# Attention body of a macaron block: ScalarE's high-part copies set back by half a key tile and more, odd chunks' loads and reciprocals a body ahead

## The reference, cut to what matters

```
x = x + 0.5 * ffn(layernorm(x))
x = x + attn(layernorm(x))
x = x + 0.5 * ffn(layernorm(x))
# attn: 32 query heads of 16 over 8 key/value heads, signs of the weights as weights
scores = einsum('bhqd,bhkd->bhqk', q, k) / sqrt(16);  out = softmax(scores) @ v
y = einsum(out, sign(o_weight)) * (s * o_scale);  nan_to_num(y, posinf=1e6, neginf=-1e6)
# ffn: x @ W_base.T + b_base + top-2-of-8 LoRA experts
```

## Time and profile before

| what | value |
| --- | --- |
| median of 3 runs | 1164.61 us (1161.82 to 1164.77) |
| profiled execution, time | 1162.41 us |
| its span | 1160.6 us |
| mean granted TensorE clock | 0.957 of 2.4 GHz |
| busy: PE, DVE, ACT, POOL | 1064.6, 837.7, 726.6, 295.9 us |

### The profile page before, as it was taken

How to read it: one execution, slowest core, us unless ns; L and a number is a source line. 1 busy time by engine, 2 the same in 40 slices (tenths; PEclk the granted TensorE clock), 3 DMA queues, 4 the chain that set the end, 5 groups by cost and what they waited for, 6 DMA issues and landing times.

```text
span 1160.6 us, 16020 instructions
## 1 busy us (share of the span) xinstructions
PE 1064.6 (92%) x5776; PEld 468.4 (40%) x5776; DVE 837.7 (72%) x1107; ACT 726.6 (63%) x1361; POOL 295.9 (25%) x485
## 2 busy tenths in 40 slices
PE   5989887999999999999999999999999999998647
PEld 4778661344334432333334333433343334233336
DVE  5766679767776777776888688777877887871274
ACT  5556433757865786675676667666766675768321
POOL 5356546302410250410050024003200320041010
PEclk9989886999999998999999999999999999999869
DMA  7122331021211123011311120121113110301300
GB/s 254 37 90 89 99 104 48 27 74 35 63 36 40 33 60 111 30 32 35 101 31 31 55 81 31 31 87 48 31 31 106 31 38 23 105 12 34 115 0 37
DMA packets 70507, 68.31 MB, mean 59 GB/s; under 512 B 15132, under 2 KB 52508, under 8 KB 70428
## 3 DMA queue, kind: packets, MB, share of 16 engines
q1 hardware_dynamic: 70172, 67.15, 18.8%
q10 hardware_dynamic: 256, 0.13, 0.0%
HBM read 41.95 MB, written 24.63 MB: 57 GB/s over the span
## 4 chain that ended last, share of the span: by engine, by line
PE 73%; DVE 13%; ACT 5%; issue 3%; POOL 3%; DMA 1%; SPq 1%; ACTq 0%; DVEq 0%; POOLq 0%
PE ps_out L1524 19%; PE ps_score L1512 18%; PE ps_max L1493 16%; PE ps_fill L1449 5%; DVE neg_max L1320 5%; PE ps_fill L1478 3%; ACT probs L1018 2%; PE ps_fill L1431 2%; PE ps_fill L1453 1%; DVE neg_max L1117 1%; DVE zd L1191 1%; PE ps_fill L1417 1%; PE ps_out L1449 1%; PE ps_fill L1423 1%; PE ps_score L1449 1%
## 5 line engine op out<-in xcount | busy, mean ns | idle before, releaser
L1018 ACT ACTIVATE probs<-ps_score 128x512 f32<-128x512 f32 x992 | 538.9, 597 | 263.4 <-PE ps_score L1512 262.3
L1320 DVE TENSOR_REDUCE neg_max<-ps_max 128x1 f32<-128x1024 f32 x480 | 570.6, 1218 | 181.1 <-PE ps_max L1493 179.1
L1512 PE MATMUL ps_score<-qst,kst 99*128 99x512 bf16 x992 | 309.5, 387 | 9.8 <-ACT probs L1018 8.2
L1493 PE MATMUL ps_max<-kst,qst 96*128 96x512 bf16 x1024 | 289.7, 389 | 16.8 <-DVE neg_max L1117 5.9
L1524 PE MATMUL ps_out<-probs,v_ring 128*32 128x512 f32 x2048 | 275.3, 609 | 7.1 <-ACT o_sb L1027 4.7
L1512 PEld LDWEIGHTS ps_score<-qst,kst 99*128 99x128 bf16 x992 | 76.2, 97 | 274.6 <-ACT probs L1018 231.7
L1493 PEld LDWEIGHTS ps_max<-kst,qst 96*128 96x128 bf16 x1024 | 91.1, 99 | 143.9 <-issue 18.7
L852 POOL CAST shift<-neg_max 128x16 bf16<-128x16 f32 x32 | 9.5, 298 | 436.7 <-DVE neg_max L1320 432.3
L1524 PEld LDWEIGHTS ps_out<-probs,v_ring 128*32 128x32 f32 x2048 | 41.0, 108 | 96.0 <-issue 87.6
L948 ACT ACTIVATE xn<-xc,ln_shift,rstd 128x512 f32<-128x512 f32 x48 | 38.6, 814 | 30.9 <-POOL ln_shift L748 19.9
L1449 PE MATMUL ps_fill<-wb_h,xt_h 128*128 128x512 f32 x84 | 46.8, 557 | 0.9 <-DVE xc L1307 0.8
(11 more groups left out here) (254 smaller groups left out, 1299.2 us busy)
## 6 DMA issues: line engine op xcount, KB each, us to landing
qst<-q_dram SPq DMA_DIRECT2D x192, 64.0 KB, 2.2
att_dram<-o_sb SPq DMA_DIRECT2D x31, 256.0 KB, 2.1
q_dram<-zm SPq DMA_DIRECT2D x24, 256.0 KB, 2.6
kst<-k_dram SPq DMA_DIRECT2D x192, 32.0 KB, 2.2
xc<-x SPq DMA_DIRECT2D x8, 512.0 KB, 3.7
x_dram<-xc SPq DMA_DIRECT2D x8, 512.0 KB, 2.9
xc<-x_dram SPq DMA_DIRECT2D x8, 512.0 KB, 5.2
out<-xc SPq DMA_DIRECT2D x8, 512.0 KB, 3.1
```

What stands on the lines that cost most here:

```text
L1018: act.activation(probs[:, kt % 2, j, :], score_bank(i, uu, j), ACT.Exp, scale=1.0 / HD ** 0.5).then_inc(probs_ready, 1)
L1320: dve.tensor_reduce(neg_max[:, uu % 2, t:t + 1], ps_max[max_slot(uu, pos)][:, :, :], AXY, ALU.max, negate=True).then_inc(max_read, 1)
L1493: last = pe.matmul(ps_max[slot][:, half, :], qst[0:SR, r, j, q * P:(q + 1) * P], kst[0:SR, r, half * 512:half * 512 + 512], start=True, st ...
L1512: pe.matmul(score_bank(i, uu, j), kst[0:SR + PARTS, uu, kt * P:(kt + 1) * P], qst[0:SR + PARTS, uu, j, :], start=True, stop=True).then_inc ...
```

## The change

In `BACK`, the two multiplications of VectorE stand on two lines behind each other. ScalarE's copy gets names of its own, `H0a` and `H0b`, and stands on later lines, and VectorE's subtractions stand behind those. The lines of all other steps are as before. The tail takes the new list too.

```diff
-    8 * [""] + ["NR", "NL", "", "", "", "", "", "N0a", "N0al N0b", "N0bl", "", "Oa0", "Oa1", "C0", ...
+    8 * [""] + ["NR", "NL", "", "", "", "", "", "N0a", "N0b H0a", "N0al", "H0b", "N0bl Oa0", "Oa1", "C0", ...
...
+LINES = 2 * UB * KT
+EVEN_SHIFT = 0
+EARLY = {"NR": 54, "NL": 57}
...
-        def back_plan(chunk):
-            return {k: [(chunk, step) for step in line] for k, line in enumerate(BACK)}
+        def back_plan(i):
+
+            plan = {}
+            for n in range(max(i - 3, 0), min(i - 1, LOOP_BACKS - 1) + 1):
+                for k, line in enumerate(BACK):
+                    for step in line:
+                        at = LINES * (n + 2) + k + (EVEN_SHIFT if n % 2 == 0 else 0)
+                        if n % 2 == 1 and step in EARLY:
+                            at = LINES * (n + 1) + EARLY[step]
+                        if at // LINES == i:
+                            plan.setdefault(min(at % LINES, LINES - 2), []).append((Chunk("back", 0, n), step))
+            return plan
...
-                    if slot == 2 and load_next is not None:
+                    if slot == 2 and load_next is not None and load_next.n % 2 == 0:
                         if load_next.n > 0:
                             sp.wait_ge(filler_ready[0], Chunk("back", 0, load_next.n - 1).written("T1b"))
                         load_att(load_next)
-                    if slot == 4 and load_next is not None:
+                    if slot == 24 and load_next is not None and load_next.n % 2 == 0:
+                        if load_next.n > 0:
+                            sp.wait_ge(att_low_ready[0], 2 * load_next.n)
+                        load_att(Chunk("back", 0, load_next.n + 1))
+                    if load_next is not None and slot == (8 if load_next.n % 2 else 4):
                         load_x1(load_next, chunk_loaded[0])
...
-                if pos in ("N0a", "N0b"):
+                if pos in ("H0a", "H0b"):
                     t = 0 if pos.endswith("a") else 1
                     act.wait_ge(att_normed[s], n * 2 + (t + 1))
                     act.activation(xt_h[s][:, :, t * P:(t + 1) * P], att_t[ch.att][:, :, t * P:(t + 1) * P],
```

More of the change, by code:

```diff
@@ L50 @@
 BACK = [s.split() for s in (
-    8 * [""] + ["NR", "NL", "", "", "", "", "", "N0a", "N0al N0b", "N0bl", "", "Oa0", "Oa1", "C0", "Ob0", "Ob1", "", "G0 C1", "P0", "", "G1", "P1",
+    8 * [""] + ["NR", "NL", "", "", "", "", "", "N0a", "N0b H0a", "N0al", "H0b", "N0bl Oa0", "Oa1", "C0", "Ob0", "Ob1", "", "G0 C1", "P0", "", "G1", "P1",
     "ADD", "", "LN1a", "LN1b", "", "LN1c", "LN1d", "T1a", "T1al", "", "T1b", "T1bl", "", "RT", "", "RU",
@@ L681, in _ @@
                 ch = Chunk("back", 0, i - 2)
-                body(i, back_plan(ch), ch)
+                body(i, back_plan(i), ch)
             ch = Chunk("back", 0, 5)
-            body(7, back_plan(ch), ch, last=True)
+            body(7, back_plan(7), ch, last=True)
             for ch in tail:
@@ L897, in _ @@
             for i in range(2, 7):
-                body(i, back_plan(Chunk("back", 0, i - 2)))
-            body(7, back_plan(Chunk("back", 0, 5)), last=True)
+                body(i, back_plan(i))
+            body(7, back_plan(7), last=True)
             for item in tail_steps():
@@ L1050, in _ @@
             for i in range(2, 7):
-                body(i, back_plan(Chunk("back", 0, i - 2)))
-            body(7, back_plan(Chunk("back", 0, 5)))
+                body(i, back_plan(i))
+            body(7, back_plan(7))
             copy_out(8, -1)
```

## The result

The changed kernel takes 1152.92 us, the median of 8 runs (1148.59 to 1159.02). The kernel before takes 1162.12 us on the same chip (8 runs, 1159.94 to 1164.77). The ratio is 0.9919, with a 95% interval of 0.9892 to 0.9946: 9.2 us, or 0.8%. The profiled execution of the changed kernel took 1151.19 us, with a span of 1149.4 us (before 1160.6) and a mean granted clock of 0.960.

The account below looks back on a forecast made before the run. TensorE's queue was taken to set the pace. Gains of 4.5 + 2.9 + 0.3 + 0.7 = 8.4 us took the profiled 1162.4 to 1154.0; the median's 2.2 us more gave 1156.2, range 1151.5 to 1161.

Parts of the forecast that it names:

- The order, bodies 3 to 7: Slots 8 and 9 of bodies 3 to 7: the reordered steps save 0.9 us a body, 4.5 in all.
- Body 2: Slots 8 and 9 of body 2: slot 10 starts 2.9 us sooner, with late sums unchanged and the clock staying up.
- the rival of the low clock: Body 2 keeps the half clock: its gain is 1.3 us, the total gain 6.8, the time 1157.8; 17%.
- The early steps: Odd chunks' loads and reciprocals a body early: 0.3 us saved in bodies 3, 5 and 7, no cost in slot 27.
- the slower rival: Slot 27 of bodies 2, 4 and 6: the early reciprocal waits for its sums, giving 1168 us; 4%.
- The tail: Chunk 7, after the bodies: VectorE's 0.70 us idle for ScalarE's copy goes, saving 0.7 us; bounds 0 and 0.7.
- All of the excess goes: Slots 8 and 9, bodies 2 to 7: VectorE is not the next limit, 15.3 us saved in all, 1149.3; 7%.
- A wait takes the other's place: Slot 9: late `copy_rows` and delayed `exp` eat most of the gain, under 3.5 us stay, 1162; 11%.

Follow-up runs that it names:

- the experiment with both: The changed kernel with the first subtraction behind `copy_rows` in all chunks and odd chunks' products a slot earlier; 1152.42 us, ratio 0.9927.

## Why the prediction was right

It said 1156.2 us with 1151.5 to 1161.0, and faster with 0.85. The time is 1152.92, inside the range, 3.3 below the forecast, and the interval of the ratio leaves out 1. The time alone could hardly tell the forecast from its rival at 1149.3, which is 3.6 away; the traces can. By the prediction's own terms:

- **The order, bodies 3 to 7: 4.5 predicted, 4.62 measured.** The route was right in the places it named. With respect to the `times_v` of slot 8, the second pair of maxima was put at 573.75 - 567.87 = 5.88 us; it is held until `copy_rows` ends, at 567.59 - 561.83 = 5.76. The copy's 0.54 us in front of slot 9's `exp` cost nothing that shows. The gain is 1.02 us in four bodies instead of 0.9, and 0.53 in body 4 for a reason the prediction hadn't: it kept the late load to body 2. That the sum came out within 0.1 us is luck: two misses of opposite sign.
- **Body 2: 2.9 predicted, 3.54 measured.** From VectorE's late product to slot 10 the prediction has 463.0 - 456.60 = 6.40 us; it is 459.94 - 453.60 = 6.34. The difference is all in the product's start, 2.45 us behind the `times_v` of slot 8 instead of 3.04. It was taken as fixed, and it depends on when the load lands. Bounds for it stood nowhere, and they should have; over ten traces it lies between 2.38 and 3.47.
- **The clock in body 2** was the one open question there. It stayed at 1.00 in both traces of the changed kernel, with idles of 0.19 and 0.85 us in the first, so the rival of the low clock, priced at 1.6 us, didn't come true in them. With ScalarE's copies moved alone the clock fell, behind idles of 1.14 and 1.45 us; in the experiment with both it stayed up, with 1.08 and 0.84, though the load landed nearly as late (3.40 us behind the `times_v` of slot 8, against 3.47). So the rival was a real one. What differs most between these two traces is the second idle, which VectorE's old order lengthens; one trace of each doesn't show that this decides, and whether the clock falls in executions that weren't profiled is not known. The Trainium skill's page "TensorE: Matmul & The Clock Gate" warns in its section "A second HAM failure mode: psum-queue depth-cycling" that short idles between groups can bring the low rate. The trace with ScalarE's copies alone agrees with that, the changed kernel's two don't show it.
- **The early steps: 0.3 predicted, 0.3 measured** in slot 5 (with them alone 2.88 in odd bodies, without them 2.98 in all). That they cost nothing in slot 27 holds too; the slower rival, a wait of the inversion for its sums, didn't come. What the prediction priced at nothing is the other end: they bring an odd chunk's inverted sums in a body ahead. Without them one of three odd bodies lost 1.27 us; in the ten traces with them no odd body waited. But the trace of before, also without them, had no such wait either, so the mean worth stays open.
- **The tail: 0.7 predicted.** The 0.70 us idle of the earlier trace rows has gone: in the tail of the changed kernel VectorE's second product and the first subtraction follow each other without a bracket.

```profile
1096.03 0.68 DVE L1277 TENSOR_TENSOR xn<-xn,zd 128x512 f32<-128x512 f32 x1
1096.63 0.68 DVE L1283 TENSOR_TENSOR xt_l<-xn,xt_h 128x512 fp32r<-128x512 f32 x1
```

  But from the last `times_v` to the end it is 72.30 us against 72.64, and in the five traces whose tail has one and the same list this stretch lies between 71.2 and 73.3. Whether the 0.7 arrives at the end is open.
- **All of the excess goes** is refuted, and the wait for VectorE, which was its counter-argument, is what is left: 0.76 us a body. The early products and the later subtractions take 0.62 of it in odd bodies (slots 8 to 10, 11.52 to 10.90).
- **A wait takes the other's place** holds of either edit by itself, and not of both. Two chains lead to the maxima of slot 9, and they are nearly of one length. With ScalarE's moved alone, VectorE's gives 6.03 us; with VectorE's alone, ScalarE's gives 6.04; before they hurt each other (6.41); with both it is 5.09. The parts give 0.10 and 0.37 us a body and the whole 1.02. That the second ScalarE copy waited as well (0.27 us in the trace of before, for the second product) was not seen in the prediction; the copy no longer waits with VectorE's order alone, and the maxima come 0.37 us sooner.

The terms for bodies 2 to 7 sum to 7.7 us predicted and 8.46 measured in the profiled pair. The miss of 3.3 us in the time is another sum. 2.5 us of it is the starting point: the forecast is 1164.61, the median of the three runs shown, less 8.4, and eight runs have their median at 1162.12. The other 0.8 us is the gain, 9.2 us by the medians instead of 8.4, and the interval of the ratio allows 6 to 13 for it. The profiled pair differs by 11.2 us, but 1.6 of that is a clock in body 1 (below) and 0.8 the start, which are no part of the change. The prediction's narrower bounds, 1153.5 to 1158.5, don't follow from its terms: 0.7 to 1.2 us a body gives 1154.7 to 1157.2. And its lower sum of 3.8 us leaves out the 0.3 of the early steps.

## What to carry to other kernels

When an engine that works its queue off in order idles for another, in front of work that a third one needs, look for the second chain that ends at the same place before pricing the fix. Here each half of the reordering gave a tenth or a third of what both gave, and the wait of the one simply came back as a wait of the other. And a use that stands just behind the landing of a load is worth moving even where the first trace shows no wait: before, the bodies behind body 2 had none, and three of the later traces had one of 0.28 to 1.18 us; three lines later there was none in the one trace taken.

## What the runs showed of the hardware

**The clock after one and the same idle.** In body 1, slots 2 and 3, TensorE idles 1.48 us for VectorE's low part, in every kernel, since nothing there is changed. The timelines of before and of the changed kernel, and the windows of slots 2 and 3 of before, of the changed kernel, and of the changed kernel's second profile:

```profile
328.15 1.04 PE L1417 MATMUL ps_fill<-ident,xn 128*128 128x128 f32 x4 [1.48 <-DVE xt_l L1273]
```

```profile
327.34 0.65 PE L1434 MATMUL ps_fill<-ident,xn 128*128 128x128 f32 x4 [1.49 <-DVE xt_l L1290]
```

```profile
324.20:333.69 9.49, 8.01 (x38) 2.57 (x37) 4.93 (x6) 5.34 (x12) 2.51 (x2) 0.82 0.00 0
```

```profile
323.39:331.25 7.86, 6.38 (x38) 2.19 (x37) 4.93 (x6) 5.29 (x12) 2.51 (x2) 1.00 0.00 0
```

```profile
324.84:334.32 9.48, 8.00 (x37) 2.56 (x37) 4.92 (x6) 5.33 (x12) 2.51 (x2) 0.82 0.00 0
```

Behind an idle of the same length the granted clock was 1.00 in one execution and on average 0.82 in the other, with the same instructions before it, and it costs 9.48 - 7.86 = 1.6 us. The last two rows are one kernel. Over twelve traces it fell in four: before, ScalarE's copies alone, VectorE's order alone, and the changed kernel once more. So the length of the idle alone doesn't tell whether the clock falls.

Body 7 has a second such place. In slot 17 TensorE idles 1.11 us for `copy_out` in every trace. In three of the twelve the clock fell to 0.50 for some 3 us: the changed kernel once more, the early steps alone, and the even chunks later. The slot then takes 3.63 us (changed kernel once more, TensorE's timeline) instead of 2.62:

```profile
1035.24 1.77 PE L1541 MATMUL ps_out<-probs,v_ring 128*32 128x512 f32 x8 [1.11 <-ACT o_sb L1044]
```

But the idle of 1.10 us in slot 9, with ScalarE's copies alone, left the clock at 1.00 in all of bodies 3 to 7. In body 2 the clock fell within or behind single idles of 2.18, 2.47 and 2.72 us and behind a pair of 1.14 and 1.45, and stayed up behind pairs of 1.08 and 0.84 and shorter, one or two traces each. Single profiles of one kernel differ by 1.6 us for body 1 and by 1.0 for body 7 from this alone.

**The landing of a load.** Body 2's inverted sums are loaded at the same place in before, the changed kernel and all experiments but the ones that leave the load out or move its user. VectorE's product started 3.04 us behind the `times_v` of slot 8 before, 2.45 and 2.38 in the changed kernel's two profiles, 3.47 with ScalarE's copies alone and 3.40 in the experiment with both, each time straight from the wait for the load; the other five traces lie between. In the later bodies it is mostly in time (late in three of the twelve traces, once in each), and which body is late differs between two profiles of one kernel (body 4 by 0.40 us in the first of the changed kernel, none in the second). What sets it isn't settled here.
